# Cross attention with head pairs per 32 rows, unpadded keys and queries, and maxima subtracted by one-row bf16 products

## What is computed

```python
def _L0_xattn_ref(x, y, Wq, bq, Wkv, bkv, q_gamma, q_beta, k_gamma, k_beta, Wproj, bproj):
    # DIM 256, H = 16 heads of D = 16; x: 64 rows a batch, y: 256 rows a batch
    q = (x @ Wq.T + bq).reshape(B, N, H, D).transpose(0, 2, 1, 3)
    kv = (y @ Wkv.T + bkv).reshape(B, M, 2, H, D).transpose(2, 0, 3, 1, 4)
    k, v = (kv[0], kv[1])
    q = _layernorm(q, q_gamma, q_beta) * SCALE
    k = _layernorm(k, k_gamma, k_beta)
    attn = jax.nn.softmax(jnp.einsum('bhnd,bhmd->bhnm', q, k), axis=-1)
    out = jnp.einsum('bhnm,bhmd->bhnd', attn, v)
    out = out.transpose(0, 2, 1, 3).reshape(B, N, C)
    return out @ Wproj.T + bproj
...
x = x + _L0_xattn_ref(_layernorm(x, axis=-1), ctx_1024, ...)
x = x + _L0_attn_ref(_layernorm(x, axis=-1), ...)
x = x + _L0_ffn_ref(_layernorm(x, axis=-1), ...)
```

## Time and profile before

| | us |
|---|---|
| median of 3 runs | 1391.31 |
| lowest, highest run | 1389.77, 1400.05 |
| the profiled execution | 1382.54 |
| its span, first to last instruction | 1380.7 |

### The profile page before, as it was taken

One profiled execution on the slowest core, in us unless ns is written; L12 is line 12 of the kernel. 1 busy time (PEld: TensorE's weight loads), 2 busy tenths in 40 slices (PEclk: granted clock), 3 DMA queues, 4 the chain that ended last, 5 costly groups with the idle time before them and its releaser, 6 DMA issues.

```text
span 1380.7 us, 54869 instructions
## 1 busy us (share of the span) xinstructions
PE 1240.6 (90%) x22808; PEld 1024.0 (74%) x22808; DVE 984.4 (71%) x2498; ACT 698.1 (51%) x1377; POOL 450.4 (33%) x436
## 2 busy tenths in 40 slices
PE   3789999999999999999999999999999986699950
PEld 3677878888888878788878787888888864488840
DVE  7458777777777777777777777777777763365547
ACT  1345555555555555555555555555555542255520
POOL 1322333333333333333333333333333222155530
PEclk7789999999999999999999999999999998699985
DMA  4100111111111111103111100111111002586558
GB/s 155 39 21 4 48 49 49 49 49 49 49 49 51 56 44 51 34 30 100 33 34 33 36 29 28 34 33 34 34 38 33 15 14 63 157 245 188 163 188 262
DMA packets 82579, 92.12 MB, mean 67 GB/s; under 512 B 17248, under 2 KB 72544, under 8 KB 82016
## 3 DMA queue, kind: packets, MB, share of 16 engines
q1 hardware_dynamic: 70816, 65.41, 16.4%
q0 software_dynamic: 6912, 19.01, 3.8%
q10 hardware_dynamic: 4608, 4.20, 0.9%
HBM read 61.19 MB, written 33.78 MB: 69 GB/s over the span
## 4 chain that ended last, share of the span: by engine, by line
PE 82%; DVE 9%; issue 4%; DMA 2%; ACT 1%; POOL 1%; SPq 0%; DVEq 0%; POOLq 0%; ACTq 0%
PE ringB L489 16%; PE ringC L500 14%; PE oA L582 10%; PE banksS L565 9%; DVE mx L1220 6%; PE banksS L783 5%; PE banksS L529 4%; PE ringB L663 3%; PE ringB L617 2%; PE ringB L649 2%; PE banksS L634 2%; PE ringB L484 2%; DMA out<-ksq 2%; PE oA L489 2%; PE banksS L544 2%
## 5 line engine op out<-in xcount | busy, mean ns | idle before, releaser
L863 ACT ACTIVATE pt<-banksS 128x1024 f32<-128x1024 f32 x128 | 127.7, 1023 | 129.6 <-PE banksS L565 118.0
L1039 POOL TENSOR_TENSOR kn<-kc,rr 128x512 f32<-128x512 f32 x64 | 66.6, 1062 | 336.0 <-DVE rr L1208 336.0
L500 PE MATMUL ringC<-wx_kv,ct 128*128 128x256 f32 x512 | 159.9, 312 | 13.6 <-DVE ws_down L1362 6.2
L1220 DVE TENSOR_REDUCE mx<-banksS 128x8 f32<-128x2048 f32 x64 | 146.3, 2287 | 0.9 <-PE banksS L544 0.9
L500 PE MATMUL ringC<-wx_kv_rest,ct 128*128 128x256 f32 x512 | 146.8, 287 | 0.0
L500 PE MATMUL ringC<-wx_kv,ct_rest 128*128 128x256 f32 x512 | 146.0, 285 | 0.0
L1033 POOL TENSOR_TENSOR sc<-sc,rz 128x1024 f32<-128x1024 f32 x32 | 62.3, 1948 | 223.5 <-DVE rz L1281 223.5
L565 PE MATMUL banksS<-qT,kT 17*128 17x64 f32 x4096 | 132.4, 278 | 0.9 <-DVE qT L1225 0.9
L565 PEld LDWEIGHTS banksS<-qT,kT 17*128 17x128 f32 x4096 | 123.5, 191 | 7.9 <-issue 1.4
L500 PEld LDWEIGHTS ringC<-wx_kv,ct 128*128 128x128 f32 x512 | 99.3, 194 | 27.6 <-DVE pos_u L1338 7.8
L1234 DVE RECIPROCAL rz<-oA 128x128 f32<-128x128 f32 x64 | 61.3, 957 | 55.5 <-PE oA L582 55.5
(11 more groups left out here) (219 smaller groups left out, 2957.0 us busy)
## 6 DMA issues: line engine op xcount, KB each, us to landing
ct_in<-in_ctxT SPq DMA_DIRECT2D x64, 256.0 KB, 3.1
pt<-rows_by_expert SPq DMA_DIRECT2D x80, 130.0 KB, 2.4
rows_by_expert<-in_pad_rows SPq DMA_DIRECT2D x16, 260.0 KB
xt<-in_x SPq DMA_DIRECT2D x32, 128.0 KB, 3.5
rows_without_experts<-base SPq DMA_DIRECT2D x32, 128.0 KB
pt<-expert_rows SPq DMA_DIRECT2D x16, 256.0 KB, 4.1
kn<-expert_rows SPq DMA_DIRECT2D x16, 256.0 KB, 4.2
out<-ksq ACTq DMA_DIRECT2D x32, 128.0 KB, 3.8
```

The costliest lines, as they stand in the source:

```text
L500: mm = pe.matmul(ringC[:, half * DIM:(half + 1) * DIM], left[:, p, k, j // 2, (j % 2) * P:(j % 2 + 1) * P], right[:, k, part * DIM:(part + ...
L863: act.activation(pt[:, g, :, :, :, :].rearrange("p i q c n -> p i (q c n)"), banksS[:, :, g * 256:(g + 1) * 256], ACT.Exp)\
L1039: pool.tensor_tensor(kn[:, 2 * jj:2 * jj + 2, :, 0:HD].rearrange("p j h d -> p (j h) d"), kc[:, 2 * jj:2 * jj + 2, :].rearrange("p j (h d) ...
L1220: dve.tensor_reduce(mx[:, 2 * r:2 * r + 2, :, HD].rearrange("p q i -> p i q"), banksS[:, :, :].rearrange("p i (q m) -> p i q m", q=2), AX. ...
```

## The change

Heads are kept in pairs per 32 rows. `kn` and `qn` lose their padding, so KT takes 8 transposes and QT 2, and `keys_in` 2 activations of 1024 columns. `queries_in` writes the queries block diagonally with four activations of 256 columns: for each pair of heads 128 columns, 64 with the even head's rows (the scale and bias of the odd rows are zero) and 64 with the odd head's. R0 and R1 take 8 matmuls each (32 rows, 128 stationary, 256 moving). The 17th row goes: `shifted` writes minus the turned maxima as bf16 into `shift16`, and C0 and C1 begin with four bf16 matmuls of one row (128 stationary columns of ones, 512 moving), one per row group, onto which 16 fp32 matmuls (32 rows, 128 stationary, 128 moving) accumulate. The set-up loses the memsets of `kn` and `qn`. Behind the loop, buffers for the last sums and for rows at rest are laid onto other tiles in the same number.

```diff
-        cols = sb("cols", [P, 9])
+        cols = sb("cols", [P, 11])
...
-        qn = sb("qn", [P, H, PAD])
-        kn = sb("kn", [P, 4, H, PAD])
+        qn = sb("qn", [P, DIM])
+        kn = sb("kn", [P, 4, DIM])
...
-        kT = sb("kT", [P, QG, 2 * M])
-        qT = sb("qT", [P, QG, P])
-        kT16 = sb("kT16", [P, QG, 2 * M], BF16)
-        qT16 = sb("qT16", [P, QG, P], BF16)
-        mx = sb("mx", [P, QG, H // QG, PAD])
-        pt = sb("pt", [P, G, H // QG, 2, 2, N])
+        kT = sb("kT", [P, G, 2 * M])
+        qT = sb("qT", [P, QG, 2 * N])
+        kT16 = sb("kT16", [P, G, 2 * M], BF16)
+        qT16 = sb("qT16", [P, QG, 2 * N], BF16)
+        mx = sb("mx", [P, QG, 4, 32])
+        shift16 = sb("shift16", [P, QG, 2 * N], BF16)
+        pt = sb("pt", [P, G, 4, 2, 2, N])
...
-        yg = [t.rearrange("p (c k d) -> p c k d", c=DEEP, k=2)
-              for t in (weighted_rows, kn[:, :, :, :].rearrange("p j h d -> p (j h d)"))]
+        yg = [t[:, 2 * c * DIM:2 * (c + 1) * DIM].rearrange("p (k d) -> p k d", k=2) for t, n in (
+                  (weighted_rows, DEEP), (kn[:, :, :].rearrange("p j d -> p (j d)"), 2),
+                  (ct_in[:, :, :, :].rearrange("p k b m -> p (k b m)"), 2)) for c in range(n)]
...
-                   qn[:, :, :].rearrange("p h d -> p (h d)"), v2[:, :, :, :].rearrange("p h o d -> p (h o d)"),
-                   qm[:, :, :].rearrange("p q n -> p (q n)"))
+                   qn[:, :], v2[:, :, :, :].rearrange("p h o d -> p (h o d)"),
+                   qm[:, :, :].rearrange("p q n -> p (q n)"), wa_o[:, :, :].rearrange("p k d -> p (k d)"),
+                   jmix[:, :, :].rearrange("p q n -> p (q n)"), xt[:, :])
...
-                for q4 in range(QG):
-                    mm = pe.transpose(oA[:, q4 * P:(q4 + 1) * P], qn[:, 4 * q4:4 * q4 + 4, :].rearrange("p h d -> p (h d)"), ident[:, :])
+                for g in range(G):
+                    mm = pe.transpose(oA[:, g * P:(g + 1) * P], qn[:, g * P:(g + 1) * P], ident[:, :])
...
-                for q4 in range(QG):
+                for g in range(G):
...
-                        mm = pe.transpose(banksS[:, q4, j * P:(j + 1) * P],
-                                          kn[:, j, 4 * q4:4 * q4 + 4, :].rearrange("p h d -> p (h d)"), ident[:, :])
+                        mm = pe.transpose(banksS[:, g, j * P:(j + 1) * P], kn[:, j, g * P:(g + 1) * P], ident[:, :])
...
-                for half in range(2):
-                    q4 = 2 * r + half
-                    for b in range(2):
-                        for i in range(4):
-                            lo = 32 * i
-                            mm = pe.matmul(banksS[b * N:(b + 1) * N, i, half * M:(half + 1) * M], qT16[lo:lo + HD, q4, b * N:(b + 1) * N],
-                                           kT16[lo:lo + HD, q4, b * M:(b + 1) * M], start=True, stop=True)
+                for b in range(2):
+                    for i in range(4):
+                        lo = 32 * i
+                        mm = pe.matmul(banksS[:, i, b * M:(b + 1) * M], qT16[lo:lo + 32, 2 * r + b, :],
+                                       kT16[lo:lo + 32, r, b * M:(b + 1) * M], start=True, stop=True)
...
-                for q4 in range(QG):
+                for i in range(4):
+                    lo = 32 * i
+                    down_by = shift16[lo:lo + 1, :, :].rearrange("p (g b) n -> p g b n", g=G)[:, :, b, :]
+                    pe.matmul(banksS[:, i, :].rearrange("p (g c n) -> p g c n", g=G, c=2), ones16[lo:lo + 1, :],
+                              down_by.unsqueeze(2).to_broadcast([1, G, 2, 2 * N]), start=True, stop=False, skip_group_check=True)
+                for g in range(G):
...
-                        at = (2 * q4 + mc) * N
+                        at = (2 * g + mc) * 2 * N
...
-                            lo, hi = 32 * i, 32 * i + HD + 1
-                            mm = pe.matmul(banksS[:, i, at:at + N], kT[lo:hi, q4, b * M + mc * P:b * M + (mc + 1) * P],
-                                           qT[lo:hi, q4, b * N:(b + 1) * N], start=True, stop=True)
+                            lo = 32 * i
+                            mm = pe.matmul(banksS[:, i, at:at + 2 * N], kT[lo:lo + 32, g, b * M + mc * P:b * M + (mc + 1) * P],
+                                           qT[lo:lo + 32, 2 * g + b, :], start=False, stop=True, skip_group_check=True)
...
-                                mm = pe.matmul(oA[32 * p4:32 * p4 + 32, at:at + N], left, pt[:, g, 2 * (p4 % 2) + odd, p4 // 2, mc, :],
+                                mm = pe.matmul(oA[32 * p4:32 * p4 + 32, at:at + N], left, pt[:, g, p4, mc, odd, :],
...
-                act.activation(qT16[:, :, :].rearrange("p q n -> p (q n)"), oA[:, :], ACT.Identity,
-                               bias=cols[:, 1:2], scale=cols[:, 0:1])
-                act.activation(qT[:, :, :].rearrange("p q n -> p (q n)"), oA[:, :], ACT.Identity,
-                               bias=cols[:, 1:2], scale=cols[:, 0:1]).then_inc(free["QT"].sem, 1)
+                for dst in (qT16, qT):
+                    for odd in range(2):
+                        ins = act.activation(dst[:, :, odd * N:(odd + 1) * N], oA[:, 0:DIM].rearrange("p (q n) -> p q n", n=N), ACT.Identity,
+                                             bias=cols[:, 2 * odd + 1:2 * odd + 2], scale=cols[:, 2 * odd:2 * odd + 1])
+                ins.then_inc(free["QT"].sem, 1)
...
-                act.activation(kT16[:, :, :].rearrange("p q m -> p (q m)"), banksS[:, :, :].rearrange("p q m -> p (q m)"), ACT.Identity,
-                               bias=cols[:, 3:4], scale=cols[:, 2:3])
-                act.activation(kT[:, :, :].rearrange("p q m -> p (q m)"), banksS[:, :, :].rearrange("p q m -> p (q m)"), ACT.Identity,
-                               bias=cols[:, 3:4], scale=cols[:, 2:3]).then_inc(free["KT"].sem, 1)
+                act.activation(kT16[:, :, :].rearrange("p q m -> p (q m)"), banksS[:, 0:G, :].rearrange("p q m -> p (q m)"), ACT.Identity,
+                               bias=cols[:, 5:6], scale=cols[:, 4:5])
+                act.activation(kT[:, :, :].rearrange("p q m -> p (q m)"), banksS[:, 0:G, :].rearrange("p q m -> p (q m)"), ACT.Identity,
+                               bias=cols[:, 5:6], scale=cols[:, 4:5]).then_inc(free["KT"].sem, 1)
...
-                pool.tensor_tensor(kn[:, 2 * jj:2 * jj + 2, :, 0:HD].rearrange("p j h d -> p (j h) d"),
+                pool.tensor_tensor(kn[:, 2 * jj:2 * jj + 2, :].rearrange("p j (h d) -> p (j h) d", d=HD),
...
-            dve.memset(kn[:, :, :, :], 0.0)
...
-            dve.tensor_scalar(cols[:, 0:2], cols[:, 0:2], HD ** -0.5, None, ALU.mult)
+            dve.tensor_scalar(cols[:, 0:4], cols[:, 0:4], HD ** -0.5, None, ALU.mult)
...
-            dve.memset(qn[:, :, :], 0.0)
...
-                dve.tensor_tensor(qn[:, :, 0:HD], qc[:, :].rearrange("p (h d) -> p h d", d=HD),
+                dve.tensor_tensor(qn[:, :].rearrange("p (h d) -> p h d", d=HD), qc[:, :].rearrange("p (h d) -> p h d", d=HD),
...
-                dve.tensor_reduce(mx[:, 2 * r:2 * r + 2, :, HD].rearrange("p q i -> p i q"),
+                dve.tensor_reduce(mx[:, 2 * r:2 * r + 2, :, 0].rearrange("p q i -> p i q"),
...
-                dve.tensor_tensor(qT[:, :, :].rearrange("p q n -> p (q n)"), oA[:, :], qT[:, :, :].rearrange("p q n -> p (q n)"), ALU.add)\
+                dve.tensor_scalar(shift16[:, :, :].rearrange("p q n -> p (q n)"), oA[:, :], -1.0, None, ALU.mult)\
...
-    def per_head(v, beyond=0):
-        return np.tile(np.concatenate([v, [beyond], np.zeros(HD - 1)]), H // QG).reshape(P, 1)
+    def per_head(v, of=None):
+        m = np.tile(v, (P // HD, 1))
+        if of is not None:
+            m[1 - of::2] = 0
+        return m.reshape(P, 1)
...
-            [per_head(a["L0_xattn_q_gamma"]), per_head(a["L0_xattn_q_beta"]),
-             per_head(a["L0_xattn_k_gamma"]), per_head(a["L0_xattn_k_beta"], -1), in_mix.reshape(P, 1),
+            [per_head(a["L0_xattn_q_" + n], of) for of in range(2) for n in ("gamma", "beta")] +
+            [per_head(a["L0_xattn_k_gamma"]), per_head(a["L0_xattn_k_beta"]), in_mix.reshape(P, 1),
```

8 lines of the change are left out of this document (4 added, 4 removed).

## The result

| | us |
|---|---|
| before, median of 4 runs (lowest, highest) | 1391.34 (1389.77, 1400.05) |
| after, median of 4 runs (lowest, highest) | 1326.35 (1323.34, 1330.75) |
| ratio, with its 95% interval | 0.9523 (0.9482 to 0.9565) |
| predicted | 1347, range 1322 to 1392 |
| the profiled execution after, and its span | 1323.34, 1320.9 |

The change makes the kernel 65 us faster, 4.8%, where 43.9 us were forecast. The span of the two profiled executions falls by 59.8 us, from 1380.7 to 1320.9.

The account below looks back on a forecast made before the run. PE, busy 90% of the span, was taken to bound the kernel. Scores 1.38, keys 0.25 and queries -0.28 gave 1.35 us a step, 32 times 43.2, plus 0.7 set-up: 43.9 off 1391.3, so 1347 us, range 1322 to 1392.

Parts of the forecast that it names:

- Scores: Score calls C0 and C1 on PE: weight loads set the pace, a call takes 1.25 us for 1.94, sparing 1.38 a step.
- the one-row products one after another: Rival in the score calls: the four one-row matmuls run in sequence, 0.65 us more a call, 1389 us in all; 12%.
- load and stream in turns: Rival in the score calls: load and stream of one row group alternate, 0.222 us a batch, 1404 us in all; 6%.
- two row groups at a time: Rival in the score calls: only two row groups stream fp32 at once, a call 2.31 us, 1415 us in all; 8%.
- Keys turned: Key transposes up to X1: eight fewer spare PE 0.91 us, but X1 waits for DVE's division, so 0.25 a step is gained.
- Queries and ACT: From QT to L663's successor: ACT's four activations set the stretch, 3.47 us for 3.19, losing 0.28 a step.
- Sum of a step: Gains and losses of one loop step added: 1.38 + 0.25 - 0.28 = 1.35 us.
- Edits at nothing: Key copies on ACT, R0 and R1, maxima, shift, scaling: costed at no gain; R1 worth at most 0.1 us.
- Set-up: Ahead of the loop: dropping or shrinking the memsets of `kn` and `qn` saves 0.7 us once, between 0.3 and 2.2.
- 32 times: Whole loop: all steps last about as long, so 1.35 us a step is gained 32 times, 43.2 us.
- The scale: 43.9 us taken off the runs' median of 1391.3 gives 1347; off the profiled execution's 1382.5, 8.8 lower, 1338.6.
- more is gained: Rival: X1 does not wait for DVE, 1326 us, or ACT's four activations cost no more than two, 1331; 12%.

Follow-up runs that it names:

- Experiment 2: The changed kernel with each fp32 score matmul of 128 moving columns cut into two of 64 with the same stationary operand; 1411.2 us, ratio to before 1.0132.
- experiment 3: The changed kernel with each transpose of the keys issued twice, 16 instead of 8, onto the same place; 1331.3 us, ratio to before 0.9581.
- experiment 8: The changed kernel, unchanged, run and profiled a second time; 1329.6 us, span 1327.7.
- experiment 1: The kernel before, unchanged, run and profiled a second time; 1392.8 us, span 1391.0.
- experiment 12: The changed kernel with, for tile 0 alone, keys turned twice and each of ACT's two key copies made in 8 pieces; 1331.6 us, ratio to before 0.9545.

## Why the prediction was right, and where it was short

The direction and the mechanism of the step held, and its terms by 0.15 or better; the size was short by 21 us of 65, and the measured 1326.35 lies near the low end of the range, which had been put there for a rival that did not occur. By its own steps:

**Scores.** Forecast: batch 0.113, the four one-row products 0.22 side by side, a call 1.25 with 0.13 around. Measured: 0.99 for 8 batches with what stands around them, 0.23, a call 1.22. Two calls spare 1.44 for 1.38. Of the rivals, the one-row products one after another (0.87), load and stream in turns (1.78) and two row groups at a time (1.74) all fall by these two rows. The rule of the Trainium skill that was weighed there falls too. The Trainium skill, "TensorE: Matmul & The Clock Gate", Part 3, has a weight load overlap a running matmul only in another row group, and the records of one row group here have 128 columns to load and 128 to stream, yet a batch takes 0.99 / 8 = 0.12. Experiment 2 gives 1.83 / 16 = 0.114 a batch. The Trainium skill, "TensorE: Matmul & The Clock Gate", Part 2, section on LDWEIGHTS, has a load take the number of columns divided by 1.2 in ns; for 128 columns that is an estimate of 107 ns, which the 114 ns here come near to.

**Keys turned.** Forecast: X1 1.56 behind KT, 0.25 gained, 0.66 turned into a wait for `oT`. Measured: 1.64 with an idle time of 0.54 released by `oT`; and experiment 3. X1 itself then takes 0.94 to the next product, for 0.87 before, so 0.10 net was gained, not 0.25.

**Queries and ACT.** Forecast: four activations 1.84 from the first start to the start behind them, L663's successor at 3.47 after QT, 0.28 lost. Measured: 720.98 - 719.17 = 1.81, 3.45, 0.26 lost. L668 itself, no longer held up by the second `probs_in`, takes 0.98 for 1.11, 0.13 gained that no term had.

**Sum of a step.** Forecast 1.35. Measured 1.44 + 0.10 - 0.26 + 0.13 = 1.41, and 33.92 - 32.51 = 1.41 as undisturbed steps. The mean over the 29 steady steps fell by 1.51; the 0.1 more are the irregular gaps, which differ from one execution to the next (1.62 between experiments 1 and 8). The forecast "a step of about 33.0 us" was 32.5 undisturbed and 32.85 on average.

**Edits at nothing.** `keys_in` on ACT was costed at nothing because PE doesn't wait there. That is right for the steady step, and wrong for the first tile, where PE waited 2.44 us for what stands behind it, and for the second, where it waited 1.92 (0.53 each after the change). R1 kept its time, 0.67 to the next product in both, which waits for ACT there. The shift took 0.69, as before.

**Set-up.** Forecast 0.7. The first MT came 3.2 earlier: 0.7 from the memset (the first reduction starts at 4.44 for 5.08), and 2.5 from the first tile's keys. This step asked only about memsets; it should have walked the first tile's own chain, in which nothing is hidden.

**The step that failed: "32 times".** The sum multiplied the gain of a steady step by 32 and took the earlier trace rows to say that all steps last about as long. In length they nearly do: the first two of the kernel before took 33.35 and 37.02 us, and a steady one 34.36 on average. But they are not the same steps. Fewer tiles are under way in them, so there is less work, and a third of their time stood at half clock; the two made up for each other, and the digits 789 behind the first 7 of the clock line in the earlier trace rows were the sign of it. After the change, at full clock, they take 24.87 and 30.73. From the 14.8 us, 2 x 1.4 are the step's own gain and 12 remain. 1.5 of these are ACT's shorter key copies in the second tile. About 10 are the clock: that is what the pieces at half clock show, and at the 0.47 us of experiment 8 the 24 us would make 11.3. So the missing term is the granted clock, and it was not in the sum at all. Why the change raises it stays open.

**The scale.** The profiled execution before lay 8.8 us under its median, the one after 3.0 under its own. The medians differ by 65.0 where the profiled executions differ by 59.2; the other 5.8 us are the choice to move the sum from one scale to the other as it stands. The profiled execution before was a fast one of its kernel, above all in its steady steps (34.36 us, for 34.65 in experiment 1).

Put together: 43.9 forecast; less 1.35 for the 32nd step, whose place is behind the last MT; 2.5 for the first tile; 12.1 for the first two steps; 4.8 for 29 steps of 1.51 instead of 1.35; -2.1 behind the last MT: 59.9 of the span's 59.8. With the scale it makes 65.

The rival "more is gained" named the right total, 1326 to 1331, for reasons that did not occur: X1 did wait, and ACT's four activations did cost more than two.

## What to carry to other kernels

Small fp32 products over four row groups, with 128 stationary and 64 to 128 moving columns, were paid by the weight load here, so fill the moving side before counting multiplications: two heads in 32 rows, half of them zeros, cost half. A gain "times the number of steps" holds for the steady steps alone; cut the trace at one recurring line and look at the first steps and their clock by themselves, and walk the first tile's chain, and the second's, where work that is hidden later is not. Steps of the same length need not have the same work or the same clock. Before an instruction is moved ahead of a wait, read the slack of everything it is moved past: the counts ahead of X1 gained 0.2 us a step, the row places ahead of the sums lost 18 us.

## What the runs showed of the hardware that was not expected

- Half clock in the early steps depends on the kernel and not on chance alone: 23 to 24 us in four profiles of the kernels with padded keys, 0 to 14 in ten of the others. In experiment 12 PE had more idle time in that stretch than in the kernel before (busy 22.77 and 24.53 of the 30 us from 45 on, though a busy time also grows at half clock), and a longer gap ahead of it (4.70 us for 2.44), and its clock stood higher, 0.89 for 0.83. The Trainium skill, "TensorE: Matmul & The Clock Gate", Part 1, explains falls by idle gaps of the engine. By that rule experiment 12 should have had at least the falls of the kernel before; it had a quarter of them. Of its two falls one, 46.3 to 49.7 us, does stand right behind the gap of 4.70; the kernel before had 10.3 us at half from 58.1 on, with no gap over 1.5 us in the 13 us ahead of them.
- A us at half clock costs nearly half a us: 3.1 us for 6.6 in experiment 8, about 10 for 24 in the kernel before. What it does not slow are the waits for other engines.
- An activation with a scale and a bias for each row costs ACT 1.81 / 4 = 0.45 us for 256 columns where 512 took 0.67: splitting one into two costs 0.24.
- The weighted products have irregular gaps, up to 0.9 us from one start to the next between 150 and 1000 us in both kernels and up to 1.4 in experiment 2. On average they make a step 0.44 us longer than an undisturbed one in the kernel before and 0.34 after (0.65 and 0.53 in experiments 1 and 8). Most of those over 0.2 us (17 of 18 before, 12 of 13 after) follow within 2.5 us on transfers of the queue that brings instructions, and only 45% of all the time does. That goes together; that the one causes the other was not tried.
- An engine may go on late behind PE: by the profile ACT does so 1.4 us after the start of the product that it waits for in experiment 2, and 0.3 in the changed kernel. Whether the signal is late or something else holds ACT is open.
